# One vector product per expert, its sum moved to GpSimd, and a re-planned order, in a four-layer decoder kernel on one core

## The reference

```python
# moe1: the two largest router probabilities, dropped past a capacity, give w (zero elsewhere)
hidden = jax.nn.silu(gate) * up
out = jnp.einsum('ech,ehd->ecd', hidden, down_w)
out = out * wbuf[:, :, None]
combined = jnp.zeros((T + 1, D)).at[dispatch.reshape(-1)].add(out.reshape(-1, D))
# moe3
h = jax.nn.silu(gate) * up
e_out = jnp.einsum('beti,eid->betd', h, Wd)
out = jnp.einsum('bte,betd->btd', weights, e_out)
```

## Time and profile before

| | |
|---|---|
| median of three runs | 1834.8 us |
| the profiled execution's own time | 1828.59 us |
| its span, first to last instruction | 1826.9 us |
| PE busy | 1387.8 us (76%) |
| DVE busy | 1102.6 us (60%) |
| ACT busy | 704.8 us (39%) |
| POOL busy | 365.9 us (20%) |
| mean granted clock of PE | 0.854 |

### The profile page before, as it was taken

How to read it: one execution, slowest core, us unless ns; L and a number is a source line. 1 busy time by engine, 2 the same in 40 slices (tenths; PEclk the granted TensorE clock), 3 DMA queues, 4 the chain that set the end, 5 groups by cost and what they waited for, 6 DMA issues and landing times. The chain is left out here.

```text
span 1826.9 us, 25724 instructions
## 1 busy us (share of the span) xinstructions
PE 1387.8 (76%) x9530; PEld 662.0 (36%) x9530; DVE 1102.6 (60%) x2350; ACT 704.8 (39%) x988; POOL 365.9 (20%) x432
## 2 busy tenths in 40 slices
PE   2668888774663676684777998889799899987886
PEld 1333432331330342342233545434344444444443
DVE  3677746778669468667976556664224524256655
ACT  1026654453333213112434452445625435433342
POOL 2415441006105106105531030112301200020000
PEclk6669987886576897696788999999899899988998
DMA  8612113000100210213122142130301401031111
GB/s 186 126 42 54 37 36 70 3 1 1 35 1 1 63 41 24 56 44 63 28 50 50 40 91 58 57 77 2 92 2 35 105 25 59 1 83 41 36 30 45
DMA packets 49784, 86.35 MB, mean 47 GB/s; under 512 B 13686, under 2 KB 42166, under 8 KB 44982
## 3 DMA queue, kind: packets, MB, share of 16 engines
q1 hardware_dynamic: 49662, 84.71, 19.7%
HBM read 66.95 MB, written 15.60 MB: 45 GB/s over the span
## 5 line engine op out<-in xcount | busy, mean ns | idle before, releaser
L1355 DVE TENSOR_REDUCE MX<-ps 128x3 f32<-128x462 f32 (+5 forms) x704 | 411.7, 627 | 215.7 <-PE ps L943 149.0
L1766 ACT ACTIVATE WORK<-ps 128x1024 f32<-128x1024 f32 (+1 forms) x352 | 312.0, 948 | 119.7 <-PE ps L971 82.4
L937 PE MATMUL ps<-KH,QH 48*128 48x154 bf16 (+5 forms) x1536 | 146.6, 279 | 124.6 <-DVE MX L1355 80.3
L1010 PE MATMUL ps<-WORK,VA 128*18 128x512 f32 (+3 forms) x1536 | 167.9, 533 | 4.8 <-ACT WORK L1774 2.0
L937 PEld LDWEIGHTS ps<-KH,QH 48*128 48x128 bf16 (+1 forms) x1536 | 61.3, 99 | 289.4 <-DVE MX L1355 156.7
L971 PE MATMUL ps<-QH,KH 54*128 54x512 bf16 (+3 forms) x768 | 120.6, 368 | 48.0 <-ACT WORK L1766 36.9
L2006 POOL TENSOR_SCALAR_AFFINE_SELECT WORK<-WORK 128x256 f32<-128x256 f32 (+1 forms) x192 | 94.6, 499 | 303.1 <-ACT WORK L1766 302.8
L2016 POOL TENSOR_TENSOR SIDE<-SIDE 128x2048 f32<-128x2048 f32 x16 | 96.5, 6034 | 292.7 <-ACT SIDE L1835 251.4
L1860 ACT ACTIVATE SIDE<-ps 128x512 f32<-128x512 f32 x96 | 57.2, 597 | 248.3 <-PE ps L1131 247.9
L1601 DVE TENSOR_TENSOR SIDE<-SIDE,ps 128x512 f32<-128x512 f32 x96 | 65.8, 687 | 122.4 <-ACT SIDE L1860 122.2
L1137 PE MATMUL ps<-SIDE 128*128 128x128 f32 x768 | 107.7, 285 | 38.8 <-DVE SIDE L1612 19.8
(11 more groups left out here) (270 smaller groups left out, 2180.5 us busy)
## 6 DMA issues: line engine op xcount, KB each, us to landing
SIDE<-in_experts SPq DMA_DIRECT2D x96, 192.0 KB, 2.4
scratch<-HQ SPq DMA_DIRECT2D x48, 192.0 KB, 2.9
QH<-scratch SPq DMA_DIRECT2D x48, 192.0 KB
SIDE<-in_wide SPq DMA_DIRECT2D x8, 1024.0 KB, 6.0
QH<-scratch SPq DMA_DIRECT2D x48, 128.0 KB
scratch<-HK SPq DMA_DIRECT2D x16, 192.0 KB, 2.9
QH<-scratch SPq DMA_DIRECT2D x48, 64.0 KB
KH<-scratch SPq DMA_DIRECT2D x16, 192.0 KB
```

What stands on the lines that cost most here:

```text
L937: mms[b] = pe.matmul(banks[b][:, c * pitch:c * pitch + width], qr[b][:, h, t * 128:t * 128 + 128], kr[b][:, h, 0:width], start=(c == 0), s ...
L1010: mm = pe.matmul(ps[32 * j:32 * j + 2 * NV, UB, q0:S], lhsT.rearrange("p a c -> p (a c)"), PB[:, (PAIR_BASE[F] + where[pi]) % NSLOT, b, at ...
L1355: dve.tensor_reduce(MX[:, 32 * b + i0:32 * b + i0 + cnt], src, AX.X, ALU.max, negate=True).then_inc(freed, 1)
L1766: act.activation(PB[:, N % NSLOT, :, lo:hi], wide_banks("pair", F, n)[:, :, lo:hi], ACT.Exp).then_inc(sem("exp_done"), 1)
```

## The change

Three things are edited.

1. In `dn`, DVE's four instructions become one `tensor_tensor` multiply of the whole bank (128x512) by w, whose one number per row tile is spread over 128 columns. Expert 0 writes ACC, the others write one of two new buffers, `WEIGHED`, by turns.
2. GpSimd adds the buffer to ACC (`add_expert`, 128x512), for every expert but the first. DVE's product of expert i, from i = 3 on, waits until the sum of expert i - 2 is done, and `acc` on PE waits for the last sum instead of for DVE.
3. The cost of `dn` in the planner changes (DVE 1.4 to 0.78, POOL 1.3 added), and with it all the planner's numbers, of which the first line is shown. The order of all five queues is written anew.

```diff
-BACKLOG, SWITCH, SOON = 3.90, 0.59, 0.153
-URGENT = {"x": 38.2, "mean": 35.7, "square": 26.1, "wo": 12.3, "mix": 35.7, "out": -10.5, "copy": 7.6, "turn": 4.3,
+BACKLOG, SWITCH, SOON = 5.04, 0.18, 0.122
+URGENT = {"x": 18.2, "mean": 40.7, "square": 30.6, "wo": 24.1, "mix": 71.7, "out": -6.5, "copy": 13.4, "turn": 9.5,
...
-        "dn": [("PE", 0.9), ("DVE", 1.4)], "acc": [("PE", 0.5), ("DVE", 0.75)],
+        "dn": [("PE", 0.9), ("DVE", 0.78), ("POOL", 1.3)], "acc": [("PE", 0.5), ("DVE", 0.75)],
...
+def sums_before(key, e):
+
+    return sum(unit[2] > 0 for unit in EXPERT_ORDER[:expert_unit(key, 0) + e])
...
+        WEIGHED = [side(at, 512).rearrange("p (t d) -> p t d", t=QT) for at in (3712, 4992)]
...
-                    consumed(pe, "dn", key, ne - 1)
+                    pe.wait_ge(sem("experts_added"), sums_before(key, ne))
                     turn(bank, [ACC[:, t, :] for t in range(QT)], W("ident")).then_inc(ring_filled, 1)
...
                 elif kind == "dn":
-                    bank = ring(kind, key, i)
-                    if i:
-                        consumed(dve, "dn", key, i - 1)
-                    for t in range(QT):
-                        o, p = ACC[:, t, :], bank[:, t * 128:t * 128 + 128]
-                        s = w[:, t, i:i + 1]
-                        if i == 0:
-                            ins = dve.tensor_scalar(o, p, s, None, ALU.mult)
-                        else:
-                            ins = dve.scalar_tensor_tensor(out=o, in0=p, scalar=s, in1=o, op0=ALU.mult, op1=ALU.add)
-                    ins.then_inc(freed, 1)
+                    n = expert_unit(key, i)
+                    bank = ring(kind, key, i).rearrange("p (t d) -> p t d", t=QT)
+                    if i >= 3:
+                        dve.wait_ge(sem("experts_added"), sums_before(key, i - 1))
+                    dve.tensor_tensor(WEIGHED[i % 2] if i else ACC, bank, w[:, :, i:i + 1].broadcast_to([128, QT, D]), ALU.mult)\
+                        .then_inc(freed, 1)
...
+            def add_expert(key, i):
+
+                if i == 0:
+                    return
+                consumed(pool, "dn", key, i)
+                if i >= 2:
+                    pool.wait_ge(sem("experts_added"), sums_before(key, i))
+                pool.tensor_tensor(ACC, ACC, WEIGHED[i % 2], ALU.add).then_inc(sem("experts_added"), 1)
+
...
+                elif kind == "dn":
+                    add_expert(key, i)
```

More of the change, by code:

```diff
@@ L145 @@
 SHAPE, RESHAPE = {"max": 64, "pair": 64, "value": 32}, 0.105
-BACKLOG, SWITCH, SOON = 3.90, 0.59, 0.153
-URGENT = {"x": 38.2, "mean": 35.7, "square": 26.1, "wo": 12.3, "mix": 35.7, "out": -10.5, "copy": 7.6, "turn": 4.3,
-          "split": 47.8, "project": -0.1, "pieces": 9.9, "send": 44.9, "max": 3.5, "hid2": 3.7, "f3": 16, "rank": 25,
[3 rows of a table removed]
-          "pair": 2, "wide": -27.3}
-STAGE_URGENT = {"moe3": -5.8, "L1x": 3.9, "moe1": 13.2, "ffn2": -10.6, "L0a": 3.3, "L2x": -0.9, "L3x": -10.9,
-          "L2a": 0.5, "self3": 47.3, "L0x": -6.8, "ffn0": 7.7, "heads1": 0.1}
-EARLIER = -0.09
+BACKLOG, SWITCH, SOON = 5.04, 0.18, 0.122
+URGENT = {"x": 18.2, "mean": 40.7, "square": 30.6, "wo": 24.1, "mix": 71.7, "out": -6.5, "copy": 13.4, "turn": 9.5,
+          "split": 41.6, "project": -4, "pieces": -7.9, "send": 54.9, "max": 5.8, "hid2": 4.5, "f3": 33.8,
[3 rows of a table added]
+          "qkv": -9.4, "pair": 3.4, "wide": -53.5}
+STAGE_URGENT = {"moe3": 17.1, "L1x": 0.6, "moe1": 34.2, "ffn2": -12.8, "L0a": 22.7, "L2x": -1.7, "L3x": -7.7, "L2a": 7,
+          "self3": 96.2, "L0x": -20, "ffn0": 44.4, "heads1": 6.6}
+EARLIER = -2.47
 def work(kind, stage, i):
```

## The result

The changed kernel takes 1854.16 us in the median of 5 runs (1850.67 to 1860.69), the kernel before 1830.84 (5 runs). The ratio is 1.0117, 95% interval 1.0094 to 1.0139. Forecast were 1819 us and a range of 1786 to 1851. The profiled execution of the changed kernel took 1860.69 us, the slowest of its five, and that of the kernel before 1828.59, so the two traces lie 32 us apart where the medians lie 23.

The account below looks back on a forecast made before the run. DVE and its hand-overs with POOL and ACT bound the middle, PE the rest; -12 + 5 + 0 - 9 = -16 us from 1828.6 gave 1812.6, or 1819 us as median; range 1786 to 1851.

Parts of the forecast that it names:

- The order, -9: New order of all queues: maxima waits saved and `heads1` batch 2 priced, net -9 us, bounds -27 and +28.
- both terms that I had priced: In the order: -14 us for maxima moved between experts of `moe1`, +5 us for `heads1` batch 2 with little PE work beside it.
- the sign that I had set: What would show the forecast: from 600 to 1000 us PE's idle time smaller and its clock higher.
- The -14 for the maxima: From 840 to 1000 us, half of PE's 27.4 us of waits for maxima or their splitting saved.
- The bound of +28: Upper bound of the order's net effect, which was taken as -9 us.
- The product, -12: DVE's product 0.44 us shorter per expert, shortening 27 PE waits of down products and maxima: -12 us, bounds 0 and -40.8.
- The bound of 0: Bound of the product's gain: nothing saved if the next hand-over, as L1601, is as late.
- The other bound, -40.8: Bound of the product's gain in us, if all 35 PE waits on L1612 go.
- The last sum, +5: PE's `acc` waits for product and POOL addition, 0.9 to 1.1 us more in each of 8 batches: +5, bounds +0.9 and +9.
- POOL's queue, 0: POOL's additions beside splittings that may stop DVE after two products: taken as 0, bounds 0 and 52 us.
- the list of five places: Five places in the order after the change where a splitting on POOL stands inside the experts, ahead of or between sums.
- The rival with DVE behind POOL: DVE stops behind POOL's splittings, two and a half of five exposed, +26 us and later turns: 1849 us, chance 0.22.

Follow-up runs that it names:

- split_ahead: Old operations, new order up to step 768, old order after, one operand splitting moved ahead of 24 causal selects in GpSimd's queue; 1.0041 of the kernel before.

## Why the prediction was wrong, step by step

**The order, -9.** This is the step that failed. It was to gain 9 us, and alone it costs 21 (1.0114 [1.0085, 1.0143]); beside it the operations make no difference that can be measured (1.0117). Some 10 us are lost in the first third, of which the prediction said nothing since no expert is there, and in the middle, where both terms that I had priced lie, an estimated 4 to 9 us are lost and not 9 gained. I counted the waits for maxima that go, and not all else that a new order of 2336 steps moves: waits for `KH<-MK`, for weights and for squares took their place. In two places steps that were ready stood behind others, on POOL and on ACT; more than half of the 21 us has no such explanation, and its cause stays open. From 600 to 1000 us PE is busy for 255.1 us where it had been for 276.5, against the sign that I had set. The -14 for the maxima looks right, since one row of PE's waits fell by 14.6 us, but that row is of the whole kernel and the forecast was for 840 to 1000 us; with the order alone it fell by 8.2. The bound of +28 covered the 21; the sum took -9.

**The product, -12.** Its size was right (689 ns for 0.69 forecast), its effect wasn't. The waits of PE's loads for it, down products and maxima, fell from 31.8 us in 27 to 25.2 in 21. Those of down products and turns fell from 36.2 us to 28.3, and not to the 24 or less that was to show it. No run has the product alone. With a sum on DVE it is 1.0003, on POOL with the splitting first 1.0022, where -12 us would be 0.993. So little of it, if any, reached the end. Which hand-over took the place of the shortened waits isn't shown. The bound of 0 named it, and was near the right end. (The other bound, -40.8, counted the 9.0 us of the turns as well; without them it is -31.8.)

**The last sum, +5.** Too high. PE's matmuls wait 6.2 us for POOL ahead of 4 of 8 turns; before, they had waited 6.3 us for DVE ahead of 6 (the 9.0 us of the earlier trace rows are the weight loads' waits). In the last batch, which nothing covers, it is 2.23 for 1.31, 0.9 more, as forecast for one batch:

```profile
1839.93 1.13 PE L1143 MATMUL ps<-SIDE 128*128 128x128 f32 x8 [0.59 <-DVE SIDE L1607]
...
1843.29 1.08 PE L865 MATMUL ps<-pack,SIDE 128*128 128x128 f32 x4 [2.23 <-POOL SIDE L2028]
```

**POOL's queue, 0.** The second step that failed. I asked what a splitting does to the sum behind it, and found, rightly, that two buffers cover it: DVE never waited for a sum. I didn't ask what the sum does to a splitting behind it. A sum waits for PE's down product and DVE; a splitting that is ready waits with it, then its transfers in SyncE's queue, then the weights behind those. In the old order that is 15 to 17 of the 21 us, by the run with the splitting first. In the changed kernel, the one that was forecast, it is less: the new order has two splittings between sums 1 and 2, in `moe1`, and moving them and the one behind the selects gives back 9 us. Those behind later sums weren't moved in any run. The rows for it were there: DVE's projections, which release POOL's splittings, and the list of five places in the new order. The rival with DVE behind POOL came to 1849 us, near the truth by luck: its mechanism didn't occur.

Of the readings of rows, one was loose: in the middle part PE's clock is at 0.5 to 0.9 and not 0.5 to 0.8. Nothing in the sum hangs on it.

## What to carry to other kernels

Before you put a new instruction in an engine's in-order queue, look at what stands behind it, not only at what it waits for and who needs its result: the queue's other work now waits for the new instruction's inputs, and so do the transfers issued behind that work. A wait for a DMA that grows in the profile is to be followed back to the queue that issued it late. And when a gain in busy time comes with a new global order, price the order by splicing: half a dozen runs told the halves apart, which the trace of before could not. Run the order alone as well as the operations alone: here each cost all of the loss, and either run by itself would have put the blame in one place.

## What the runs showed of the hardware

DVE can be held for a whole instruction of POOL. While POOL multiplies 128x2048 float32 in SBUF (5.34 us), DVE's L1443, with both inputs in SBUF, which takes 0.68 us elsewhere, takes 5.47. The rows are from `split_ahead`, with old operations and the new order up to step 768:

```profile
557.44 5.34 POOL L2049 TENSOR_TENSOR SIDE<-SIDE 128x2048 f32<-128x2048 f32 x1 [64.86 <-ACT SIDE L1868]
557.85 5.47 DVE L1443 TENSOR_TENSOR XT<-YC,RS 128x512 f32<-128x512 f32 x1
```

The two end within 0.6 us of each other. In the kernel before the instruction that met POOL there was a cast of 128x64, at 552.51, and it took 5.17 us in place of 0.19; it has a single input. The longest row of L1410 in the earlier trace rows had been 1.22 us, so its size there did not show what the next order would bring. The Trainium skill (GPSIMD Engine Reference, Key points) says that GpSimd shares its SBUF interfaces with VectorE; the trace agrees, and adds that DVE's instruction may wait until POOL's is over. Against that the 88 additions on POOL left the product with its PSUM input alone: 680 to 693 ns in all 96, of which some 30 ran beside an addition.

A spread operand cost nothing here: the product with [128, 4, 1] spread to [128, 4, 128] takes 689 ns, the plain one of the same size, L1607, 687.
